# Four recurrent and attention stages of a conditioned sequence model on one core: preparation with B and C in one product and half-sums on GpSimd, scans of twice the length, unpadded heads

## What is computed

```python
# layer 0: low-rank pairs whose matrices come from the condition
h = gelu(layernorm(c, ln_g, ln_b) @ W1 + b1);  w = h @ W2 + b2
a1, bb1, a2, bb2 = split(w)                       # each (B, 256, 8)
x = x + ((gelu((x @ a1) @ bb1^T)) @ a2) @ bb2^T
# layer 1: modulated LN, a selective state space in both directions, then an MLP
xs, z = split(h @ in_w);  xs = silu(xs)
proj = xs @ xproj_w                               # dt (512), B (64), C (64)
dt = softplus(proj_dt + dt_bias);  A = -exp(A_log)
state = state * exp(dt * A) + (dt * x_t) * B_t;  y_t = state . C_t
out = (y + xs * D) * silu(z) @ out_w              # 512 channels x 64 states, 256 steps
# layers 2 and 3: transformer blocks with modulated LN, 16 heads (of 64, then of 16), T = 256
```

## Time and profile before

| | us |
|---|---|
| median of 3 runs | 8064.74 (8062.61 to 8066.53) |
| the profiled execution | 8064.97, its span 8063.2, mean granted clock 0.954 |
| conditioning | 101.9, PE busy 77.9 |
| prepare | 840.7, PE busy 726.3, DVE 408.0, ACT 419.3, POOL 72.6 |
| scan | 4670.5, DVE busy 4624.2, ACT 4433.8, PE 3988.8 |
| finish_scan | 343.0, PE busy 308.1 |
| layer 2 | 1175.1, PE busy 1107.5 |
| layer 3 | 932.0, PE busy 863.1, DVE 482.7, ACT 456.8 |

### The profile page before, as it was taken

One profiled execution on the slowest core, in us unless ns is written; L12 is line 12 of the kernel. 1 busy time (PEld: TensorE's weight loads), 2 busy tenths in 40 slices (PEclk: granted clock), 3 DMA queues, 4 the chain that ended last, 5 costly groups with the idle time before them and its releaser, 6 DMA issues. The chain is left out here.

```text
span 8063.2 us, 233691 instructions
## 1 busy us (share of the span) xinstructions
PE 7071.7 (88%) x94272; PEld 3761.9 (47%) x94272; DVE 6189.8 (77%) x4829; ACT 5870.7 (73%) x7834; POOL 2286.7 (28%) x1375
## 2 busy tenths in 40 slices
PE   7999588888888888888888888887989999979998
PEld 5444244444444444444444444444435454535554
DVE  2555499999999999999999999998434353445554
ACT  2555499999999999999999999996224343435544
POOL 0000133333333333333333333332003232323332
PEclk9999699999999999999999999998999999989999
DMA  4666522222222222222222222222520000000000
GB/s 151 151 155 146 117 70 67 64 68 67 70 66 66 67 68 69 66 66 68 67 67 66 68 68 67 67 64 98 200 81 9 6 9 8 6 32 9 12 11 6
DMA packets 621116, 541.43 MB, mean 67 GB/s; under 512 B 490224, under 2 KB 528752, under 8 KB 606448
## 3 DMA queue, kind: packets, MB, share of 16 engines
q1 hardware_dynamic: 620032, 526.35, 22.5%
HBM read 380.72 MB, written 145.49 MB: 65 GB/s over the span
## 5 line engine op out<-in xcount | busy, mean ns | idle before, releaser
L1267 DVE TENSOR_TENSOR_SCAN s_h<-s_decay,s_h 128x1040 f32<-128x1040 f32 x2048 | 4623.9, 2336 | 33.8 <-ACT s_decay L1191 33.8
L1162 ACT COPY s_h<-s_pb 128x1024 f32<-128x1024 f32 x2048 | 2506.0, 1224 | 111.1 <-PE s_pb L1093 92.2
L1106 PE MATMUL s_py<-s_h,s_cz 128*32 128x128 f32 x32768 | 2512.9, 436 | 6.1 <-DVE s_h L1267 6.1
L1191 ACT ACTIVATE s_decay<-s_pa 128x1024 f32<-128x1024 f32 x2048 | 2139.4, 1045 | 123.6 <-DVE s_h L1267 53.4
L1234 POOL TENSOR_TENSOR s_h<-s_h,s_one 128x64 f32<-128x64 f32 x384 | 875.3, 2279 | 2079.3 <-DVE s_h L1267 2079.3
L1078 PE MATMUL s_pa<-s_dl,s_al 18*128 18x64 bf16 x32768 | 857.8, 192 | 673.7 <-ACT s_decay L1191 584.9
L1106 PEld LDWEIGHTS s_py<-s_h,s_cz 128*32 128x32 f32 x32768 | 1036.5, 123 | 469.3 <-issue 10.0
L1078 PEld LDWEIGHTS s_pa<-s_dl,s_al 18*128 18x128 bf16 x32768 | 612.8, 95 | 1019.9 <-ACT s_decay L1191 953.4
L1093 PEld LDWEIGHTS s_pb<-s_ul,s_bl 18*128 18x128 bf16 x16384 | 475.3, 95 | 1031.3 <-ACT s_h L1162 877.5
L1093 PE MATMUL s_pb<-s_ul,s_bl 18*128 18x128 bf16 x16384 | 838.1, 222 | 27.7 <-ACT s_h L1162 16.0
L1222 POOL TENSOR_TENSOR s_cz<-s_cl,s_one 128x128 f32<-128x128 f32 x256 | 434.3, 1697 | 964.2 <-PE s_py L1106 952.4
(11 more groups left out here) (223 smaller groups left out, 6219.2 us busy)
## 6 DMA issues: line engine op xcount, KB each, us to landing
s_bl<-B SPq DMA_DIRECT2D x1024, 72.0 KB
s_ul<-U SPq DMA_DIRECT2D x1024, 72.0 KB
s_dl<-D SPq DMA_DIRECT2D x1024, 72.0 KB
s_al<-A SPq DMA_DIRECT2D x256, 144.0 KB
D<-p_dp SPq DMA_DIRECT2D x64, 384.0 KB, 6.5
U<-p_up SPq DMA_DIRECT2D x64, 384.0 KB, 5.6
B<-p_bz SPq DMA_DIRECT2D x144, 128.0 KB, 2.2
SZ<-p_sz SPq DMA_DIRECT2D x16, 1024.0 KB, 5.1
```

The source lines that it names most:

```text
L1106: mm = pe.matmul(py[e % 2][QR * q:QR * q + QR, 0:P], cz[e % 2][:, l * P + QR * q:l * P + QR * q + QR], states, start=(l == 0), stop=(l == ...
L1162: act.copy(out, pb[:].rearrange("p b t d -> p d b t")).then_inc(bu_done, 1)
L1191: act.activation(decay[(STEPS * e + 2 * z + j) % RING][:, :, 1:W], pa[j % 2][:], ACT.Exp).then_inc(exp_done, 1)
L1267: dve.tensor_tensor_scan(seg, decay[(STEPS * e + 2 * z + j) % RING][:].rearrange("p d w -> p (d w)"), seg, 0.0, ALU.mult, ALU.add).then_in ...
```

## The change

Five stages are edited; `finish_scan` stays as it is.

- Conditioning: the small operand (hidden, silu, condition, padded to 32 columns) becomes the stationary side and w2a, w2b and wm the moving one, in 4 (wm: 3) column groups of the array. The results of w2a and wm are copied by ACT and transposed back on PE. The loads come in the order condition, vectors, w1, A_log, w2a, w2b, b2b, wm. The constants of `az` are set on GpSimd. The 18 stores of A3 go into `prepare`, behind its second load of weights.
- Prepare: B and C of a direction come from one product of 256-column matmuls (8 matmuls), DVE copies B rows to `brow`, PE transposes them (2 transposes). `to_bc` now stands ahead of `low2`; ACT's and PE's B work of the second direction goes to the next unit. The low-rank steps of the two sequences use partitions 0 to 7 and 32 to 39. GpSimd adds the halves of x1 and of the squares, so that mean and var are one matmul each. u is made in two instructions, one a sequence.
- Scan: one DVE instruction covers 32 rows of 65 (2080 elements), the decay ring is 3 buffers of twice the size, and the waits count these longer instructions.
- Transformer: layer 3's heads are unpadded (HR = 16, MT = 2, PT = 4); its weights are loaded as before into `hid` and repacked by DVE, ACT and GpSimd, the biases by 8 small DMAs. In both layers the filler is cut at MIDDLE = 5.

```diff
 # conditioning, PE
+                def group(out, g, j, weights, k, moving, at):
+                    return pe.matmul(out[GB * g:GB * (g + 1), j, :], weights[:, k, :],
+                                     moving[:, k, 512 * at:512 * (at + 1)], start=(k == 0), stop=(k == FC - 1))
...
-                for m in range(32):
+                for j in range(2):
                     for k in range(FC):
-                        mm = pe.matmul(pw[:, 0, m * NB:(m + 1) * NB], w2a[:, k, m * P:(m + 1) * P],
-                                       hid[:, k, :], start=(k == 0), stop=(k == FC - 1))
+                        for g in range(4):
+                            mm = group(pw, g, j, hid, k, w2a, 2 * g + j)
...
+                for j in range(3):
+                    for k in range(FC):
+                        for g in range(3):
+                            mm = group(pm, g, j, sil if g else cond, k, wm, 3 * g + j)
 # prepare, GpSimd
+                    for b in range(PAIR):
+                        cols = slice(b * T, (b + 1) * T)
+                        pool.tensor_tensor(u[:, :, cols], dt_[:, :, cols], xs[r][:, :, cols], ALU.mult
+                                           ).then_inc(s["u_done"], 1)
+                def halves(i):
+                    wait(pool, s["x1_done"], i + 1)
+                    pool.tensor_tensor(x1h[:], x1[:, 0, :], x1[:, 1, :], ALU.add).then_inc(s["x1h"], 1)
+                    wait(pool, s["sq_done"], i + 1)
+                    pool.tensor_tensor(sqh[:], sq[:, 0, :], sq[:, 1, :], ALU.add).then_inc(s["sqh"], 1)
 # prepare, PE
                 def to_bc(i, r):
...
-                    for k in range(IC):
-                        pe.matmul(g1[:, 0, :], cdup[r][:, k, :, :].rearrange("p e s -> p (e s)"), xs[r][:, k, :],
-                    for q in range(4):
+                    for b in range(PAIR):
                         for k in range(IC):
-                            mm = pe.matmul(g1[:, 1, q * S:(q + 1) * S], xs[r][:, k, q * P:(q + 1) * P],
-                                           xp_w[r][:, k, DI:DI + S], start=(k == 0), stop=(k == IC - 1))
+                            w = xp_w[r][:, k, DI:DI + 2 * S] if b else cb_w[r][:, k, :, :].rearrange("p e s -> p (e s)")
+                            mm = pe.matmul(g1[:, 0, b * T:(b + 1) * T], w, xs[r][:, k, b * T:(b + 1) * T],
...
                     to_z(i, 0, range(IC))
+                    to_bc(i, 0)
                     if more:
                         low2(i + 1)
-                    to_bc(i, 0)
+                    turn_b(i, 0)
 # scan
-    RING = 6
+    STRIDE = 2
+    HALVES = STEPS // STRIDE
+    RING = 3
-                        for j in range(STEPS):
-                            if j % (STEPS // 2) == 0:
-                                wait(dve, carried, 2 * k + j // (STEPS // 2) + 1)
-                            wait(dve, exp_done, STEPS * k + j + 1)
+                        for j in range(HALVES):
+                            if j % (HALVES // 2) == 0:
+                                wait(dve, carried, 2 * k + j // (HALVES // 2) + 1)
+                            wait(dve, exp_done, STEPS * k + STRIDE * (j + 1))
+                            rows = slice(STRIDE * FG * j, STRIDE * FG * (j + 1))
 # transformer
-    HR, dh = (DH2, DH2) if layer == 2 else (PADH, DH3)
+    HR, dh = (DH2, DH2) if layer == 2 else (DH3, DH3)
+    MIDDLE = 5
-                        project(i + 1, slice(3, 4))
+                        project(i + 1, slice(3, MIDDLE))
...
-                        project(i + 1, slice(4, 6))
+                        project(i + 1, slice(MIDDLE, MIDDLE + 2))
```

More of the change, by code:

```diff
@@ L207, in _ @@
+                pe.wait_ge(ident_set, 2)
+                pe.wait_ge(w2b_in, 16)
+                for j in range(2):
                     for k in range(FC):
-                        mm = pe.matmul(pw[0:NB, 1 + m % 3, :], hid[:, k, :], w2b[:, k, m * 512:(m + 1) * 512],
-                                       start=(k == 0), stop=(k == FC - 1))
+                        for g in range(4):
+                            mm = group(pb, g, j, hid, k, w2b, 2 * g + j)
                     mm.then_inc(bb_mm, 1)
+                for j in range(2):
+                    pe.wait_ge(war_done, j + 1)
+                    for q in range(4):
+                        mm = pe.transpose(pw[:, j, q * P:(q + 1) * P], war[:, j, q * P:(q + 1) * P], ident[:])
+                    mm.then_inc(wat_mm, 1)
@@ L418, in _ @@
                 reload(0)
+                for j in range(PARTS):
+                    for m in range(PARTS):
+                        for b in range(PAIR):
+                            sp.dma_start(scratch["A3"][:, m, j, b].rearrange("n d f -> d n f"),
+                                         keep["az"][:, :, m, b].rearrange("p n c s -> p n (c s)")).then_inc(s["a_out"], 16)
                 def unit(i, more, reads):
@@ L627, in low @@
                     wait(act, s[f"low{k}_mm"], i + 1)
-                    act.copy(lows[:, k - 1, :], ga[0:RANK, 0, :]).then_inc(s[f"low{k}_done"], 1)
+                    for b in range(PAIR):
+                        act.copy(lows[rank(b), k - 1, :], ga[rank(b), 0, 0:T]).then_inc(s[f"low{k}_done"], 1)
                 def gelu(i):
                     wait(act, s["up1_mm"], i + 1)
-                    act.activation(g[:], ga[:], ACT.Gelu).then_inc(s["gelu_done"], 1)
+                    act.activation(by_sequence(g), ga[:].rearrange("p b (m t) -> p b m t", t=T), ACT.Gelu).then_inc(s["gelu_done"], 1)
                 def square(i):
@@ L1626, in transformer @@
     PT = HT // 2
+    LEAD = HR * (PT - 1)
     VJ = VW // 512 if layer == 2 else 1
@@ L1712, in _ @@
                 load(0, 0)
-                weights(wqkv, f"Wqkv{layer}")
-                weights(wo, f"Wo{layer}")
+                if layer == 2:
+                    weights(wqkv, "Wqkv2")
+                    weights(wo, "Wo2")
+                else:
+                    unpadded()
                 weights(w1, f"W1{layer}")
@@ L1857, in _ @@
                 pe.wait_ge(s["wqkv_in"], 16)
+                if layer == 3:
+                    for n in "qkv":
+                        pe.wait_ge(s["w" + n], 1)
                 pe.wait_ge(s["h1"], 4)
@@ L1888, in slot @@
                     if first(i):
-                        pe.wait_ge(s["wo_in"], 16)
+                        pe.wait_ge(s["wo_in"], 16 if layer == 2 else 128)
                     wait(pe, s["o_done"], TILES * (i + 1))
@@ L1964, in _ @@
                 deviation1(0)
+                if layer == 3:
+                    act.wait_ge(s["wqkv_in"], 16)
+                    act.copy(*columns_of(1)).then_inc(s["wk"], 1)
                 take_v(0)
```

389 lines of the change are left out of this document (229 added, 160 removed).

## The result

The changed kernel takes 7958.5 us (median of 4 runs, 7954.33 to 7960.09) against 8064.1 of before (4 runs): a ratio of 0.9868 with a 95% interval of 0.9851 to 0.9885, 106 us or 1.3% less. I had forecast 7942 with 7860 to 8020. The profiled execution has a span of 7957.9 us and a mean clock of 0.948.

What follows compares the result with a forecast made beforehand. It took DVE to bound the scan, and chains through DVE, ACT and GpSimd to hold PE at the changed places in preparation and the transformer. Terms -75 - 49 + 6 - 11 + 6 = -123 from 8065 gave 7942 us, range 7860 to 8020.

Steps and rivals of the forecast that it cites:

- I take 75: Scan: 75 ns fixed cost saved for each of 1024 joined instructions, -77 us.
- The lower bound of 47: Scan: fixed cost of 47 ns an instruction if the recurrence runs at exactly two slopes an element, -48 us.
- The +2 for the first double: Scan: the first double-length instruction needs two exps instead of one, +2 us.
- rival 3: Scan: the exponentials become the bound, slab 18.6 us, +141 instead of -75, whole 8158 us; chance 0.04.
- Rival 5: Conditioning: the array's column groups don't run at once, -29 us, whole 7962, inside the range; no separate chance.
- +4.3 to +7: Preparation: the next dt product starts 4.3 to 7 us later in a unit.
- +14: Preparation: seven units at a middle net of +1.9 us each.
- my -8: Preparation: 4 us less at the start and 4 less in the last unit.
- the +6: Layer 3: unpadded heads add +2.5 us in seven slots, less at both ends, total +6 (-15 to +30).
- Rival 1: Preparation and layer 3: PE is the bound, its savings gained in full (-106, -84), whole 7740; 7850 or less: chance 0.09.
- Rival 2: Scan: nothing is paid per instruction, whole 8019 us; chance 0.07.
- Rival 4: Preparation and layer 3 both at their bad ends, +35 and +30 us, whole 7995; chance 0.15.

Runs made afterwards that it cites:

- e4: Changed kernel with low2 of the next unit ahead of the B and C product again: preparation 807.8 us against 834.5, whole 7930.17.
- e10: Changed kernel with u of preparation made in one GpSimd instruction of 2048 columns: preparation 853.9 us against 834.5, whole 7980.9.
- e5: Changed kernel with preparation's mean and variance from matmuls over both halves, without GpSimd's half-sums: preparation 841.4 us against 834.5, whole 7961.64.
- e8: Changed kernel with MIDDLE = 4 in both layers: layer 2 1174.8 us against 1163.0, layer 3 937.7 against 933.0, whole 7973.96.
- e9: Changed kernel with only the first q job taken by VectorE ahead of the residuals, not three: layer 3 918.5 us against 933.0, whole 7943.73.
- e1: Changed kernel with the scan back at 1040 elements an instruction and six decay buffers: scan 4670.1 us against 4626.9, whole 8003.97.
- e12: Changed kernel with carries on ScalarE, low2 first, one q job ahead of residuals, and x1 and centring earlier on DVE: preparation 808.5 us, whole 7872.76.
- e13: Kernel of e12 with, on ScalarE, the silu of z's first two columns ahead of the second dt copy: preparation 788.8 us, whole 7855.55.

## Why the prediction was right, and where it was off

The time lies in the range, and in every edited stage the limit was of the kind I named. That the sum came within 18 us (-123 against -105) is in part luck: the scan's term was too hopeful by 31, preparation's too gloomy by 12 and layer 3's by 5, and within conditioning and layer 3 wrong sizes cancelled.

- **Scan, mis-sized.** "I take 75": the fixed part measured 50 ns. I took the tensor_tensor's fixed part as the nearest row, although the recurrence has its own. My 2.227 us was also too long: 8.90/4 is 2.225, and the first of the five scans took longer (2.25 us to the next) than the others, which are 2.213 apart. The lower bound of 47 came close by luck: with 2.213 the same working leaves 33, because two slopes an element (2.096 ns) are more than the 2.08 that joining shows (4.38 - 2.213 for 1040 more). The 60 ns that the Trainium skill gives (VectorE: DVE Perf Modes, the TRN2 errata) would have made -62, nearer than mine, and still too much. The +2 for the first double is 1.8; 5 us of waits between scans came besides, 2.8 of them for carries, so DVE's idle time is 40.6, a hair over the 40 that I had set as a sign. That GpSimd's carries fit, but for these 2.8, and that ACT keeps up (rival 3) held.
- **Conditioning, right in mechanism, the sizes by luck.** In four groups w2a's records took 182 ns and w2b's 161 (171 forecast), the products of wm 7.2 us (7.7). But these are means over two rates: at full clock a step of three groups is 0.43 us, 143 ns a record where I had 213, and it took 0.83 while the clock was at 0.50. My working charged each record a fixed issue time on top of its share, and did not see the half clock behind the wait for wm; the two nearly cancelled. (w2a's steps also shorten midway, from 0.85 to 0.42 us, though the clock's record is 1.00 all along; why is open.) wm landed at 42.98 and not 38, the transposes took 1.3 and not 3.3: -46.6 for -49. Rival 5 did not happen. No run takes the parts of this stage's change apart (moving side, order of the loads, stores).
- **Preparation, right in mechanism, mis-sized a unit.** Variance came 4.3 us later behind its place in the order (I had 5.4), and the dt product behind it 3.3 later, below my +4.3 to +7. In the unit shown, variance to variance is 95.75 us (250.23 to 345.98) against 96.12 before, so the rest of the unit gave back 4.7. Over all seven steps the change is +2.3 where I had +14, of which +2.1 in the first; the two ends gave -8.5 for my -8. My own terms, +4.3 less 5, would have allowed -0.7 a unit; I wrote +0.5 as the low end. e4 shows the cause that I named, the copy of low2 behind B and C, to be worth 27 us, e10 the halves of u to be worth 19, and e5 the half-sums 7. The joint B and C product and the low-rank steps side by side were not undone by themselves.
- **Layer 2, right**: -12.1, all of it MIDDLE (e8).
- **Layer 3, right in mechanism.** The six steps between the seven slots that have a successor grew by 13 us, 2.2 each, where I had 2.5 seven times, +17; up to the first mean2 the stage gave 8.5 and not 7, and the last step 3.6. PE idles 3.96 us ahead of mean2 (3.9 forecast), 0.3 to 0.8 ahead of var2 in most slots (2.3) and 4.5 to 6 ahead of f (6). The chain through nine q and k evictions held mean2 back, as e9 shows. But I priced MIDDLE in layer 2 alone; in layer 3 it gave 4.7 (e8), and with MIDDLE = 4 the unpadded heads cost the 5.8 that the +6 says.
- **Rival 1** (PE's savings in full) did not happen: PE's busy time fell by 132 us in preparation and layer 3 together, the two stages by 5. **Rival 2** (nothing paid per instruction) is refuted by e1. **Rival 4** did not happen: both stages ended below their forecasts.
- On the drain that the Trainium skill names (TensorEngine Tiling, Key Properties): low2 in two column groups starts at 221.06, lasts 1.04, and the full-array transposes start at 222.10; no gap beyond hundredths is to be seen. No run prices it by itself.

## What to carry to other kernels

Before costing a PE saving, find what the next wait of PE is for, and cost the chain behind it: here 132 us of PE work were worth 5, while moving one product behind a short one (27 us), five evictions behind the residuals (14 us) and one activation ahead of a copy (20 us, with e12's moves on DVE in place) were worth twelve times that together. Joining two scans of 2.2 us on DVE saved some 50 ns; a spacing must be read from several instructions in mid-stream, not from the first. And a chain can have two members of like lateness: in e12 moving one showed nothing, and the gain came when the other had moved too.

## What I had not expected of the hardware

GpSimd's half-sum of 128x512 takes 1.26 us alone and 3.25 beside DVE's 2.28 us subtraction of 2048 columns; in e13 the other half-sum, with 1.29 us of such a subtraction beside it, takes 2.41. Not every DVE instruction with two inputs does this: in e12 the half-sum of x1 has 1.2 us of a 128x128 remainder beside it and takes 1.31. A GpSimd operation that waits for a DVE scan costs that scan about 0.08 us (carry) to 0.18 (fill), whether the scan is 2.2 or 4.4 us long. Putting the same carry on ACT, at 0.37 us a copy, was nearly free although ACT was busy for 95% of the scan stage (4386 of 4627 us).
